# Logits in one run, then the turned output, then four transposes: a new order of TensorE's work in an attention unit

## What is computed

```python
q, k, v = to_heads(x @ Wq), to_heads(k), to_heads(v)      # 16 heads of 64
sim = einsum('bid,bjd->bij', q, k) * 64 ** -0.5           # the logits, 2048 x 2048 per head
G = sigmoid(sim)
P = minimum(flip(cumsum(flip(G, -1), -1), -1), 63)        # position of each key as seen by a query
E = einsum('bnc,ct->bnt', q, pos_emb)                     # the position logits
w = P - floor(P)
sim = sim + w * E[ceil(P)] + (1 - w) * E[floor(P)]
out = einsum('bij,bjd->bid', softmax(sim), v)
x = layernorm(x + out @ Wout + b_out)
```

## Time and profile before

| | |
|---|---|
| median of 3 runs | 2661.84 us (2654.25 to 2664.03) |
| profiled execution | 2657.76 us, its span 2655.9 us |
| mean granted TensorE clock | 0.987 of full speed |
| TensorE busy | 2460.8 us, 93% of the span |
| VectorE busy | 2017.8 us, 76% |
| ScalarE busy | 1620.4 us, 61% |

### The profile page before, as it was taken

How to read it: one execution, slowest core, us unless ns; L and a number is a source line. 1 busy time by engine, 2 the same in 40 slices (tenths; PEclk the granted TensorE clock), 3 DMA queues, 4 the chain that set the end, 5 groups by cost and what they waited for, 6 DMA issues and landing times. The chain is left out here.

```text
span 2655.9 us, 64192 instructions
## 1 busy us (share of the span) xinstructions
PE 2460.8 (93%) x18687; PEld 1690.0 (64%) x18687; DVE 2017.8 (76%) x5179; ACT 1620.4 (61%) x3383; POOL 190.7 (7%) x289
## 2 busy tenths in 40 slices
PE   7999998999899989998999899999999988999997
PEld 5666666666566666665666566666666655777776
DVE  5888888888888888888888888888899960232322
ACT  4666666666666666666666666666666652444442
POOL 0000000000000000000000000000000000111111
PEclk9999999999999999999999999999999998999998
DMA  2010101010101010100101010101001002100100
GB/s 67 20 34 20 34 20 30 20 34 20 34 20 34 20 33 20 33 20 22 30 22 31 23 29 24 29 24 29 22 21 40 21 17 67 34 26 34 36 26 6
DMA packets 96567, 74.74 MB, mean 28 GB/s; under 512 B 24590, under 2 KB 92303, under 8 KB 96464
## 3 DMA queue, kind: packets, MB, share of 16 engines
q1 hardware_dynamic: 96464, 73.15, 10.1%
HBM read 14.26 MB, written 2.10 MB: 6 GB/s over the span
## 5 line engine op out<-in xcount | busy, mean ns | idle before, releaser
L409 ACT ACTIVATE probsT<-ring 128x512 f32<-128x512 f32 x1024 | 583.4, 596 | 580.4 <-PE ring L555 580.4
L555 PEld LDWEIGHTS ring<-ident,probs 128*128 128x128 f32 x4096 | 435.1, 141 | 567.6 <-ACT probsT L409 356.8
L555 PE MATMUL ring<-ident,probs 128*128 128x128 f32 x4096 | 617.8, 284 | 133.4 <-ACT probsT L409 131.7
L757 DVE TENSOR_REDUCE mx<-Sc 128x1 f32<-128x1024 f32 x512 | 621.5, 1214 | 141.3 <-PE Sc L547 135.0
L547 PE MATMUL Sc<-qk,q_now 64*128 64x512 f32 x2048 | 583.7, 647 | 22.8 <-issue 16.0
L430 ACT ACTIVATE probs<-Sc,nbias 128x1024 f32<-128x1024 f32 x512 | 566.8, 1122 | 4.7 <-DVE nbias L774 4.7
L569 PE MATMUL out<-probsT,V_now 128*64 128x128 f32 x8192 | 530.0, 277 | 0.0
L569 PEld LDWEIGHTS out<-probsT,V_now 128*64 128x64 f32 x8192 | 439.5, 137 | 76.2 <-ACT probsT L409 37.5
L721 DVE COPY_PREDICATED z<-mask,z 128x224 f32<-128x224 int16 (+5 forms) x768 | 386.9, 504 | 34.3
L348 POOL TENSOR_TENSOR prod<-cut,z 128x350 f32<-128x350 f32 x128 | 118.7, 927 | 2039.9 <-DVE z L744 2039.9
L547 PEld LDWEIGHTS Sc<-qk,q_now 64*128 64x128 f32 x2048 | 156.0, 186 | 111.2 <-issue 111.2
(11 more groups left out here) (116 smaller groups left out, 2288.5 us busy)
## 6 DMA issues: line engine op xcount, KB each, us to landing
q_now<-qk SPq DMA_DIRECT2D x256, 64.0 KB, 2.0
xv<-xT SPq DMA_DIRECT2D x113, 128.0 KB, 2.2
q_far<-qk SPq DMA_DIRECT2D x128, 64.0 KB, 1.9
V_now<-V SPq DMA_DIRECT2D x16, 512.0 KB, 3.2
at<-attn SPq DMA_DIRECT2D x16, 512.0 KB, 3.2
probs<-in_x_dram SPq DMA_DIRECT2D x4, 512.0 KB, 5.2
wqk<-in_L_attn_Wq_dram SPq DMA_DIRECT2D x32, 64.0 KB, 2.1
xin<-in_x_dram SPq DMA_DIRECT2D x16, 128.0 KB, 2.8
```

What stands on the lines that cost most here:

```text
L409: nc.scalar.activation(probsT[:, u, 4 * s:4 * s + 4, :], ring[k % 2][:, :].rearrange("p (t q) -> p t q", q=P), ACT.Copy).then_inc(slot_out, 1)
L555: last = nc.tensor.transpose(ring[k % 2][:, j * P:(j + 1) * P], probs[:, u, (4 * s + j) * P:(4 * s + j + 1) * P], ident[:, :])
L757: nc.vector.tensor_reduce(mx[:, u, half:half + 1], Sc[:, half * HALF:(half + 1) * HALF], AX.X, ALU.max).then_inc(dve_unit, 1)
```

## The change

It alters the order of TensorE's program in a unit, and with it the numbers of the ring fills and the order in which ScalarE empties them. Both halves of a tile's logits now follow each other. For tile 1 the window comes right behind them. Then the turned output takes the first ring buffer of the run, and then come all four transpose groups. No matmul and no copy is added or removed.

```diff
 class Slots:
     def __init__(self, first=False, proj=True):
-        self.last = [0, 1, 3, 4]
-        self.turn0 = 2
+        self.turn0 = 0
+        self.last = [1, 2, 3, 4]
         at = 6 if first else 5
         self.qk, self.values = at, at + 1
         at += 2 if proj else 0
-        self.turn1 = at + 2
-        skip = 0 if first else 1
-        self.now = [at, at + 1, at + 2 + skip, at + 3 + skip]
+        self.turn1 = at
+        at += 0 if first else 1
+        self.now = [at, at + 1, at + 2, at + 3]
...
 # ScalarE, body
                     empty_halves(g - 1, 0)
-                    transposed(1, base, at.last, (0, 1))
                     scale(g - 1, 0, base, at.turn0)
-                    transposed(1, base, at.last, (2, 3))
+                    transposed(1, base, at.last)
...
-                transposed(0, base, at.now, (0, 1))
                 if not first:
                     scale(g - 1, 1, base, at.turn1)
-                transposed(0, base, at.now, (2, 3))
+                transposed(0, base, at.now)
...
 # TensorE, body
                 logits(par, 0, 0)
                 if not first:
-                    transposes(1, base, at.last, 0)
                     wait_apart(pe, exp_done, g * 4, waited)
                 logits(par, 0, 1)
                 if not first:
-                    transposes(1, base, at.last, 1)
                     turn(g - 1, 0, base, at.turn0)
-                    transposes(1, base, at.last, 2)
-                    transposes(1, base, at.last, 3)
+                    for s in range(4):
+                        transposes(1, base, at.last, s)
                     outputs(g - 1, 1, base, at.last, tiles=range(FIRST))
...
                 logits(par, 1, 0)
-                transposes(0, base, at.now, 0)
                 wait_apart(pe, exp_done, g * 4 + 2, waited)
                 logits(par, 1, 1)
-                transposes(0, base, at.now, 1)
-                if not first:
-                    turn(g - 1, 1, base, at.turn1)
-                transposes(0, base, at.now, 2)
-                transposes(0, base, at.now, 3)
                 if far:
                     pe.wait_ge(near_out, g * 2 + 4)
                     window(g + 2, par if far_par is None else far_par)
+                if not first:
+                    turn(g - 1, 1, base, at.turn1)
+                for s in range(4):
+                    transposes(0, base, at.now, s)
                 outputs(g, 0, base, at.now, empty=not first)
```

More of the change, by code:

```diff
@@ L402, in _, with transposed @@
                     near_tanh(1)
-            def transposed(u, base, slots, part):
-                for s in part:
+            def transposed(u, base, slots):
+                for s in range(4):
                     k = slots[s]
```

## The result

The changed kernel takes **2721.5 us** (median, 2714.8 to 2725.7), the kernel before 2661.4 us: a ratio of 1.0234, with a 95% interval of 1.0205 to 1.0263. It is 60 us slower. I had forecast 2686 us, which is +24 us, so the sign is right and the size is not. The measured time lies at the very top of my range (2648 to 2722), which had been drawn that wide for another mechanism.

A forecast was written before the change was run, and what follows sets the result against it. TensorE's stream nearly ties with ring, ScalarE and exponentials. +0.24 (A) and -0.06 (B) give +0.18 us over 127 units, +23, plus 1 for the last units: 2682 profiled, 2686 us as median; range 2648 to 2722.

The forecast's parts named there:

- my range: Whole kernel: 2648 to 2722 us, holding the forecast, no change and the near part of the "Much slower" case.
- Two near ties: TensorE's stream, and behind it ring, ScalarE and exponentials: shortening one helps only as far as the other allows.
- B: Unit's second stretch, tile 1's first logits to next unit's; 8.05 us before, forecast 7.99, change -0.06.
- A: Unit's first stretch, tile 0's first logits to tile 1's; 8.62 us before, forecast 8.86, change +0.24.
- 0.92 us of switches: TensorE, per unit: two transpose groups between logits (0.16 + 0.20 each) and the window's own switch (0.20) disappear.
- The turned output's emptying, 0.43 us late: In A: ScalarE begins 0.43 us after the turned output lands, working out an address; after the change on the path.
- B ends with TensorE waiting for exponentials: End of B: TensorE is ready at 7.62 us and waits 0.37 for exponentials; next logits at 7.99.
- Logits, logits, window with no wait between: Start of B: these three run without waiting, 2.72 us until the turned output starts.
- four rivals: 2665 us (losses cancel gains, chance 0.20), 2624 (short turned-output round, 0.10), 2545 (only switches count, 0.04), 2734 (much slower, 0.12).
- Much slower: Rival: delay in B 0.36 us, some three restarts after waits 0.1 us dearer each; +0.57 per unit, 2734 us, chance 0.12.
- The forecast's own range: 2662 to 2705 us, from the delay's bounds in B and about half as much again for restarts.
- -0.16 us: Per unit, lower bound from the turned output's emptying delay in B: 0.11 us instead of the estimated 0.27.

The follow-up runs named there:

- tanh_early: far_first with ScalarE's tanh of the window ahead of its run of emptyings in B; 2635.9 us, ratio 0.9913 to the kernel before.
- group_first: Kernel before with only tile 0's half (A) regrouped, B as before; 2673.0 us, ratio 1.0047.
- fixed_place: far_first with every scaled output written to one fixed place in attn, so the layer isn't computed; 2624.7 us, ratio 0.9868 to the kernel before.
- far_first: The changed kernel with q_far loaded ahead of V_now in the first unit of a head; 2675.2 us, ratio 1.0052 to the kernel before.
- turn_late_grouped: turn_late with both logits halves in one run, four transposes in one run, window behind them; 2610.1 us, ratio 0.9805 to the kernel before.
- turn_late: Kernel before with the turned output taken out from between the transposes, logits and transposes still alternating; 2633.3 us, ratio 0.9899.

## Why the prediction was right and wrong

- *Two near ties, TensorE's stream and the chain of ring, ScalarE and exponentials.* Right: tanh_early shortens the one by 0.35 us in B and finds the other there at once, since A's second logits wait as before.
- *0.92 us of switches go, but the ring gives back more.* Right for the ordinary unit: +0.23 us measured, +0.18 predicted, each station of the table within 0.04 us. group_first (+0.16 us per unit) shows the ring's part with B untouched.
- *The turned output's emptying, 0.43 us late, comes onto the path.* Right: fixed_place takes it off and gains 50 us on far_first.
- *B ends with TensorE waiting for exponentials.* Right: tanh_early.
- *"Logits, logits, window with no wait between", in B.* **This is the step that failed.** It is true of 112 units. In the first unit of 15 heads the window waits for q_far. I had asked when q_now is reloaded, but not when q_far arrives, which the window reads; SyncE's queue doesn't occur in my working, and the term stood at nothing. far_first against the change gives the price, 46 us, of which 30.0 are the waits; 0.23 x 112 = 26 us of ordinary units is the smaller part. Without this term the kernel takes 2675 us (far_first), 11 below my 2686.
- *The range and the rivals.* None of the four rivals is this one. "Much slower" (2734 us) came near the measured time with restarts after waits in the run, which the stations of the ordinary unit refute; that it came near, and that my range, widened towards it, just holds the measured time, is luck. The forecast's own range, 2662 to 2705, doesn't hold it, and its lower end doesn't follow from the bounds that I gave: -0.16 us x 127 makes 2666, with half as much again 2655.
- *The two rules.* The Trainium skill says that a change of tiling mode drains TensorE (TensorEngine Tiling (Array Packing), Key Properties). turn_late_grouped against turn_late agrees, 23 us faster with fewer such changes. The Trainium skill also says on the same page (PSUM Bottleneck) that tiling speeds up TensorE but not the emptying of PSUM. No tiling was added here, but the ordinary unit agrees in kind: 0.92 us of switches went, and with the ring behind it it grew by 0.23 us.

## What to carry to other kernels

When an instruction is moved forward, list everything it reads and find the latest moment at which each of these arrives, in the first and last iteration of every enclosing loop too, where queues hold other work than in the steady state. An interleaving that looks like wasted mode switches may be what hides a two-buffer ring; before grouping, take out of the run whatever has a slow round on that ring. Whether work should stand ahead of a run of buffer fills or behind it depends on what waits at the run's end: the window behind it was worth 28 us while the exponentials waited for the tanh, and the window ahead belongs to the fastest order, in which the tanh had been taken out of that path.

## What was not expected of the hardware

A short stop of TensorE can be paid twice. After the stop of 2.34 us shown above, the granted clock stood at 0.58 on average over the next 3.3 us, though TensorE was busy all through them, and was full during the stop itself. All six stops of more than 2 us were followed by such a stretch, and two of the nine shorter ones, both of about 1.66 us, while five others between 1.66 and 1.70 us had none. The length of the stop alone doesn't tell them apart, and no run here shows what does.
